# A fused four-block network on one core: the last stage's order of work, rotary buffers and token split rearranged

## The reference, cut to what matters

```python
for i in range(6):
    x = attn_layer(shift_tokens(x), Wqkv[i], q_scale[i], k_scale[i], Wo[i]) + x
    x = ffn_layer(shift_tokens(x), ln_g[i], ln_b[i], W1[i], b1[i], W2[i], b2[i]) + x

def shift_tokens(t):            # the upper 64 channels come from the token before
    a, s = split(t, 2, -1)
    return concat([a, pad(s, one token)[:, :-1]], -1)

def attn_layer(x, Wqkv, qs, ksc, Wo):   # 16 heads of 64, windows of 32 tokens
    q, k, v = heads(x @ Wqkv)
    q, k = l2norm(q) * qs, l2norm(k) * ksc
    q = q * cos * scale + rotate_half(q) * sin * scale
    k = k * cos / scale + rotate_half(k) * sin / scale
    return local_attention(q, k, v) @ Wo     # softmax over own window and the one before
```

## Time and profile before

| | |
|---|---|
| median of three runs | 4209.49 us (4209.45 to 4212.79) |
| the profiled execution, its own time | 4207.12 us |
| its span, first to last instruction | 4205.3 us |
| mean granted clock of TensorE | 0.969 of full |
| TensorE busy (matmuls) | 3880.3 us, 92% |
| VectorE busy | 3528.0 us, 84% |
| ScalarE busy | 2636.6 us, 63% |
| GpSimd busy | 2381.6 us, 57% |

### The profile page before, as it was taken

How to read it: one execution, slowest core, us unless ns; L and a number is a source line. 1 busy time by engine, 2 the same in 40 slices (tenths; PEclk the granted TensorE clock), 3 DMA queues, 4 the chain that set the end, 5 groups by cost and what they waited for, 6 DMA issues and landing times.

```text
span 4205.3 us, 120168 instructions
## 1 busy us (share of the span) xinstructions
PE 3880.3 (92%) x48128; PEld 2725.0 (65%) x48128; DVE 3528.0 (84%) x5537; ACT 2636.6 (63%) x5550; POOL 2381.6 (57%) x2045
## 2 busy tenths in 40 slices
PE   3457998999995999999999999999999999999998
PEld 1225776777774676767776676666766676666765
DVE  6875556777776999999999999999999999999997
ACT  3543336666664666676667666676667666666665
POOL 0111001000002887888878788888878787888885
PEclk7768999999997999999999999999999999999999
DMA  3000000000001333233333333233332333233332
GB/s 105 0 0 1 1 1 1 1 0 0 0 0 41 75 92 82 62 84 89 78 75 70 80 90 82 62 84 91 77 78 67 80 90 82 65 81 75 84 85 65
DMA packets 264675, 238.95 MB, mean 57 GB/s; under 512 B 31716, under 2 KB 260328, under 8 KB 263400
## 3 DMA queue, kind: packets, MB, share of 16 engines
q1 hardware_dynamic: 264168, 231.82, 23.6%
HBM read 26.20 MB, written 4.19 MB: 7 GB/s over the span
## 4 chain that ended last, share of the span: by engine, by line
PE 71%; DVE 13%; ACT 7%; issue 4%; POOL 2%; SPq 2%; DMA 1%; DVEq 0%; ACTq 0%; POOLq 0%
PE bank L1990 13%; PE bank L1923 13%; PE bank L2008 8%; PE bank L1963 7%; PE bank L2050 5%; PE bank L854 4%; ACT arena L1129 3%; PE bank L1956 2%; PE bank L2063 2%; DVE arena L1016 2%; PE bank L1934 2%; DVE arena L1026 2%; PE bank L1254 1%; PE bank L1245 1%; SPq L2169 1%
## 5 line engine op out<-in xcount | busy, mean ns | idle before, releaser
L1451 DVE TENSOR_TENSOR arena<-bank,tab 128x1024 f32<-128x1024 f32 x768 | 935.4, 1218 | 179.7 <-ACT arena L1683 108.0
L1846 POOL TENSOR_TENSOR arena<-arena 128x512 f32<-128x512 f32 x768 | 1011.8, 1333 | 52.1 <-DMA arena<-arena 47.9
L1683 ACT ACTIVATE arena<-bank 128x512 f32<-128x512 f32 x768 | 458.2, 597 | 518.7 <-PE bank L1923 510.0
L1923 PE MATMUL bank<-x_split,wqk_split 128*128 128x256 f32 x4608 | 717.8, 299 | 41.9 <-DVE arena L1451 27.5
L1990 PE MATMUL bank<-m_vo,arena 128*32 128x512 f32 x6144 | 753.9, 597 | 2.1 <-DVE arena L1544 1.1
L1923 PEld LDWEIGHTS bank<-x_split,wqk_split 128*128 128x128 f32 x4608 | 603.5, 191 | 185.5 <-issue 94.4
L1854 POOL TENSOR_TENSOR arena<-arena 128x256 f32<-128x256 f32 x768 | 559.0, 739 | 152.3 <-ACT arena L1683 151.9
L1707 ACT ACTIVATE arena<-bank 128x512 f32<-128x512 f32 x768 | 457.5, 596 | 182.0 <-PE bank L1990 178.9
L1863 POOL TENSOR_TENSOR arena<-arena 128x1024 f32<-128x1024 f32 x192 | 372.8, 1942 | 240.3 <-DVE arena L1499 240.3
L1187 POOL TENSOR_TENSOR x_all<-x_all,arena 128x256 f32<-128x256 f32 x16 | 11.6, 728 | 832.6 <-DVE arena L1008 832.6
L1869 POOL TENSOR_TENSOR arena<-arena 128x1024 f32<-128x1024 f32 x192 | 372.3, 1940 | 122.7 <-DVE arena L1512 122.7
(11 more groups left out here) (258 smaller groups left out, 7115.9 us busy)
## 6 DMA issues: line engine op xcount, KB each, us to landing
arena<-arena SPq DMA_DIRECT2D x1536, 128.0 KB, 2.5
wqk_stage<-in_wqk SPq DMA_DIRECT2D x6, 1024.0 KB, 8.5
out_x<-x_all SPq DMA_DIRECT2D x7, 512.0 KB, 5.0
wvt<-in_wvt SPq DMA_DIRECT2D x6, 512.0 KB, 4.6
wo<-in_wo SPq DMA_DIRECT2D x6, 512.0 KB, 5.7
arena<-in_wbh SPq DMA_DIRECT2D x1, 2048.0 KB, 9.6
w<-in_w SPq DMA_DIRECT2D x6, 341.0 KB, 5.7
wqk_stage<-out_x SPq DMA_DIRECT2D x8, 128.0 KB, 2.4
```

What stands on the lines that cost most here:

```text
L1451: nc.vector.tensor_tensor(d_t[c % KS].rearrange("p k h t -> p k (h t)"), bank[c % 2][:, :].unsqueeze(1).to_broadcast([P, 2, 2 * T]), tab[: ...
L1683: nc.scalar.activation(d_sq[i % 4].rearrange("p h t -> p (h t)"), bank[c % 2][:, :], ACT.Square).then_inc(s_sq, 1)
L1846: nc.gpsimd.tensor_tensor(d_rot[i // 4][:, i % 4, :, :], t[:, :, 0, :], t[:, :, 1, :], ALU.add).then_inc(s_ad, 1)
L1923: last = nc.tensor.matmul(bank[c % 2][:, h * T:(h + 1) * T], wqk_split[:, i, wp, h, :], x_split[:, n % 2, xp, :], start=(q == 0), stop=(q ...
```

## The change

Five things, all in the last stage:

- TensorE's order: `project(f - 1, 5)` comes before `scores(f - 2, 0)`, and `token_products` 0, 1 and 2 stand together before `project(f, 0, 1)`.
- `KS`, the number of rotary buffers, is 4.
- The low half of the tokens is made from bank 6 (PSUM) in two pieces of 64 partitions, the second shifted by a token, at the head of VectorE's turn. It waits until the projections of pass `f - 2` are through. The first column of the second piece is zeroed once, at the start (the eighth of `ZEROS`). `attention(f - 3, 0)`, which writes bank 6, waits for it.
- VectorE's order: rotary product 3 moves to the turn before, product 5 ahead of the first maximum, product 2 ahead of the first softmax sum; the second softmax sum comes behind product 3 and the last residual; the norm's steps stand together.
- ScalarE reads token product 0 before it copies the norm's high half; in the turn of a layer's head matrices the copy comes first. GpSimd's weight splits are spread over the turn, and only two are done in the turn before a new layer.

```diff
--- before.py
+++ after.py
@@ -1316,7 +1316,7 @@
         QUADS = H // 4
         NF = len(FBLK)
         CHUNKS = 8
-        KS = 3
+        KS = 4
         d_xt = [ld(T) for _ in range(3)]
         d_sq = [ld(2, T) for _ in range(4)]
         d_t = [ld(2, 2, T) for _ in range(KS)]
@@ -1353,7 +1353,7 @@
         kept_in = wqk_stage[:, :].rearrange("p (g n c) -> p g n c", g=2, c=C)
         x_kept = [kept_in[:, 0], kept_in[:, 1], wvt[:, :, :], wo[:, :, :]]
         STORES = ((0, 4), (4, 8), (8, 12), (12, 15), (15, 16))
-        ZEROS = 7
+        ZEROS = 8
         TURNS_D = TOTAL + 4
 
         def at_least(eng, s, count):
@@ -1436,8 +1436,12 @@
                 if not here(n):
                     return
                 dve.wait_ge(s_xh, n + 1)
-                nc.vector.tensor_tensor(x_split[:, n % 2, 1, :], d_xt[n % 3], x_split[:, n % 2, 0, :].bitcast(F32), ALU.subtract)\
-                    .then_inc(s_split, 1)
+                at_least(dve, s_proj, CHUNKS * (n - 1))
+                first, second, now = slice(0, C // 2), slice(C // 2, C), n % 2
+                nc.vector.tensor_tensor(x_split[first, now, 1, :], bank[6][first, 0:T],
+                                        x_split[first, now, 0, :].bitcast(F32), ALU.subtract)
+                nc.vector.tensor_tensor(x_split[second, now, 1, 1:], bank[6][second, 0:T - 1],
+                                        x_split[second, now, 0, 1:].bitcast(F32), ALU.subtract).then_inc(s_split, 1)
 
             def rotary_products(n, *chunks):
                 if not here(n):
@@ -1590,6 +1594,7 @@
             nc.vector.scalar_tensor_tensor(d_rstd, d_wn, 1.5, d_rstd, ALU.add, ALU.mult).then_inc(s_stats, 1)
             for v in (*d_xt, d_xf):
                 nc.vector.memset(v, 0.0).then_inc(s_zero, 1)
+            nc.vector.memset(x_split[:, :, 1, 0:1].bitcast(F32), 0.0).then_inc(s_zero, 1)
             dve.wait_ge(s_stats, 8)
             dve.wait_ge(kept, 16 * (NT // KEEP))
             normalise(0)
@@ -1603,38 +1608,38 @@
             dve.wait_ge(s_zero, ZEROS)
             dve.wait_ge(s_stats, 13)
             for f in range(TURNS_D):
+                split_low_tokens(f)
                 turn_probabilities(f - 3, 1)
-                rotary_products(f - 1, 3)
+                rotary_products(f - 1, 4)
                 ffn_gate(f - 4, 0)
-                rotary_products(f - 1, 4)
+                rotary_products(f - 1, 5)
                 softmax_maximum(f - 2, 0)
-                rotary_products(f - 1, 5)
                 softmax_shift(f - 2, 0)
                 rotary_products(f - 1, 6, 7)
                 ffn_gate(f - 4, 1)
+                ffn_gate(f - 4, 2)
                 softmax_maximum(f - 2, 1)
-                split_low_tokens(f)
-                ffn_gate(f - 4, 2)
                 norm_weight(f - 1)
+                norm_factor(f - 1)
+                norm_split(f - 1)
                 residual(f - 3)
-                norm_factor(f - 1)
+                softmax_shift(f - 2, 1)
                 rotary_products(f, 0)
-                norm_split(f - 1)
-                softmax_shift(f - 2, 1)
                 scale_keys(f - 1, 0)
                 rotary_products(f, 1)
                 scale_keys(f - 1, 1)
+                rotary_products(f, 2)
                 softmax_sum(f - 2, 0)
-                rotary_products(f, 2)
                 ffn_weight(f - 3)
                 softmax_reciprocal(f - 2, 0)
                 ffn_factor(f - 3)
                 ffn_scale(f - 3)
-                softmax_sum(f - 2, 1)
-                softmax_reciprocal(f - 2, 1)
+                rotary_products(f, 3)
                 if f - 4 == LAST:
                     add_kept(3, SEQS - 4, SEQS - 1)
                 ffn_residual(f - 4)
+                softmax_sum(f - 2, 1)
+                softmax_reciprocal(f - 2, 1)
                 turn_factors(f - 1)
                 turn_probabilities(f - 2, 0)
                 if f < 2:
@@ -1787,6 +1792,7 @@
             for f in range(TURNS_D):
                 fresh = here(f) and f % SEQS == 0
                 next_fresh = here(f + 1) and (f + 1) % SEQS == 0
+                turned = here(f - 2) and (f - 2) % SEQS == 0
                 read_products(f - 3, 7)
                 read_tokens(f)
                 split_high_tokens(f)
@@ -1807,13 +1813,22 @@
                     weights_high(layer_of(f), 6)
                 nc.scalar.preload_act_table_set(EXP_SET)
                 norm_rsqrt(f - 1)
-                if here(f - 2) and (f - 2) % SEQS == 0:
+                if turned:
                     head_matrices(layer_of(f - 2))
-                softmax_exp(f - 2, 0)
-                squares(f, 0)
-                norm_high(f - 1)
-                read_products(f - 2, 0, 1, 2)
-                squares(f, 1)
+                if turned:
+                    norm_high(f - 1)
+                    squares(f, 0)
+                    softmax_exp(f - 2, 0)
+                    squares(f, 1)
+                    read_products(f - 2, 0, 1, 2)
+                else:
+                    read_products(f - 2, 0)
+                    norm_high(f - 1)
+                    softmax_exp(f - 2, 0)
+                    read_products(f - 2, 1)
+                    squares(f, 0)
+                    read_products(f - 2, 2)
+                    squares(f, 1)
                 if fresh and f:
                     weights_high(layer_of(f), 7)
                 ffn_tokens(f - 3)
@@ -1883,14 +1898,21 @@
                 rotary_sums(f - 1, 5)
                 scale_shifted(f - 2, 0)
                 rotary_sums(f - 1, 6, 7)
+                if fresh:
+                    split_low(pool, layer_of(f), 2, 3)
                 scale_shifted(f - 2, 1)
+                add_halves(f, 0, 1)
                 if fresh:
-                    split_low(pool, layer_of(f), 4, 5, 6, 7)
-                add_halves(f, 0, 1, 2, 3)
+                    split_low(pool, layer_of(f), 4, 5)
+                add_halves(f, 2, 3)
+                if fresh:
+                    split_low(pool, layer_of(f), 6)
                 softmax_scale(f - 2, 0)
+                if fresh:
+                    split_low(pool, layer_of(f), 7)
+                if next_fresh:
+                    split_low(pool, layer_of(f + 1), 0, 1)
                 softmax_scale(f - 2, 1)
-                if next_fresh:
-                    split_low(pool, layer_of(f + 1), 0, 1, 2, 3)
 
         def phase_d_tensor(pe):
             def turn_tokens(n):
@@ -1999,6 +2021,7 @@
                 pe.wait_ge(s_uev, NW * n + 4 * h + 4)
                 if h == 0:
                     pe.wait_ge(s_xt, min(n + 4, TOTAL))
+                    pe.wait_ge(s_split, min(n + 4, TOTAL))
                     if n + 3 > LAST:
                         pe.wait_ge(s_x_done, n - 1)
                 for r in range(QUADS):
@@ -2094,8 +2117,8 @@
                 turn_tokens(f)
                 ffn_up(f - 4, 0)
                 ffn_up(f - 4, 1)
+                project(f - 1, 5)
                 scores(f - 2, 0)
-                project(f - 1, 5)
                 attention(f - 3, 0)
                 project(f - 1, 6)
                 ffn_up(f - 4, 2)
@@ -2108,10 +2131,10 @@
                     head_matrices(layer_of(f - 2))
                     project(f, 0, 1)
                 token_products(f - 2, 0)
+                token_products(f - 2, 1)
+                token_products(f - 2, 2)
                 if not turned:
                     project(f, 0, 1)
-                token_products(f - 2, 1)
-                token_products(f - 2, 2)
                 ffn_tokens(f - 3)
                 spread_norms(f - 1, 0)
                 token_products(f - 2, 3)
```

## The result

The changed kernel takes 4258.98 us (median of 5 runs, 4246.59 to 4267.75), the kernel before 4212.79 us beside it (5 runs, 4209.45 to 4217.12): ratio 1.0106, 95% interval 1.0092 to 1.0120. It is 46 us slower, where 58 us less were forecast. The profiled execution took 4267.75 us, 60.6 more than that of before; its span is 60.7 longer than the earlier trace rows.

What follows compares the result with a forecast made beforehand. A loop over TensorE, VectorE and GpSimd was taken as the bound: 91 turns x 28.68 + 15.7 = 2625.6 us, 58.5 under 2684.06, giving 4148.6 profiled and 4151 median; range 4106 to 4196.

Steps and rivals of the forecast that it cites:

- the third rival: VectorE's norm split misses its place behind GpSimd's sum, making every turn 1.23 us longer: 4263 us, chance 7%.
- S: Start of TensorE's sum of squares in a turn, from which the forecast counted its chain of waits.
- step 4: VectorE from rotary product 2 to the second reciprocal, with the moved operations between: 6.25 us, ending at S + 17.35.
- step 5: GpSimd from the second reciprocal through scaling, rotary sums and halves: 11.26 us, plus 0.07 to hand over.
- The loop: Chain over TensorE, VectorE and GpSimd between successive sums of squares, taken as the new turn: 28.68 us.
- Step 1: TensorE's sum of squares, attention and three token products (0.43, 1.75, three at 0.86); chunk 0 starts at S + 4.76.
- Steps 2 and 3: Chunk 0 to rotary product 0 in 1.57 us, then VectorE's operations and chunk 2's squares; product 2 at S + 11.10.
- The switch at chunk 5 and attention: TensorE's new order avoids slow starts after 32-column products: 0.20 us saved at chunk 5, 0.13 at attention.
- the wait at chunk 4: TensorE's wait for VectorE's rotary product 2 goes: 0.13 + 0.23 = 0.36 us a turn.
- the other 0.33: TensorE's saving from grouped token products (0.13 us) and from tokens' transposes following the projection (0.20).
- The low half: VectorE's two pieces from PSUM take 0.8 us in place of the removed subtraction's 1.35; alone this gains nothing.
- The splits at new layers: GpSimd's spread weight splits give back 2.05 us in each of five new-layer turns: 10.3.

Runs made afterwards that it cites:

- e1: Changed kernel with the norm's weight put in PSUM, so that the factor reads one SBUF tensor: 4240.43 us, ratio 1.0061.
- e11: e5 with TensorE's order as in the kernel before, six stretches of full products: 4240.66 us, ratio 1.0065.
- e5: Changed kernel with the norm's factor and split both reading PSUM, and one more copy on ScalarE: 4186.57 us, ratio 0.9944.
- e10: Kernel before with only the tokens' low half made from PSUM in two pieces, with the zeroed column and attention's wait: 4216.60 us, ratio 1.0014.
- e3: Kernel before with only GpSimd's weight splits in the changed kernel's places: 4202.01 us, ratio 0.9975.
- e4: Changed kernel with the tokens' low half subtracted in one piece from the SBUF copy, at its new place: 4298.08 us, ratio 1.0202.
- e12: Changed kernel with GpSimd's first scaling of scores ahead of rotary sum 5: 4259.85 us, ratio 1.0110.
- e2: Changed kernel with the residual between the norm's weight and factor, so the factor is asked for later: 4262.17 us, ratio 1.0121.
- e8: Changed kernel with GpSimd's rotary sums 6 and 7 waiting for the norm's split: 4232.61 us, ratio 1.0055.

## Why the prediction was wrong, point by point

**The step that failed** is the rejection of the third rival: "Against: 1.35 and 0.45 show that VectorE gets in at the next boundary." The kernel before showed that in each of its turns, and it is no rule. In the change the factor meets GpSimd's queue with 0.6 us of the scaling left and with two sums ready behind it, and is passed over by both in half of the turns (3.36 us for 0.88). The sum had no term for this wait, and only 7% was given to it. That the rival's time (4263) lies near the measured 4259 is luck: it took 1.23 in every turn, and the runs show 1.64 in about half of them and another 0.31 in every turn that has nothing to do with the lock. Its place was one instruction off as well: the factor stalls, while the split stalls only in e1, where the factor no longer does. I had looked at the factor as one that "waits until S + 3.4". It is done at S + 3.26 in the short turn (2120.76 to 2124.02) and at S + 5.74 in the long one.

How the 112.7 us between the forecast's 2625.6 and the 2738.29 divide: 47 long turns at 1.64 are 77; the short turn's length, 28.99 for 28.68, is 91 x 0.31 = 28; the 8 left are four middle turns, the factors of 4.7 and new layers. The 0.31 is 0.24 in steps 1 to 3, 0.03 in step 4 and 0.04 in step 5.

**The loop, step by step,** against the short turn's chain (S = 2120.76):
- Step 1: 4.92 for 4.76. The sum of squares took 0.54 for 0.43 and the three products 2.64 for 2.58.
- Steps 2 and 3: product 0 starts 1.58 behind chunk 0 (1.57 forecast), product 2 another 4.84 later (4.77). Product 2 starts at S + 11.34 for S + 11.10.
- Step 4: from product 2 to the second reciprocal's row in the chain 6.28 (2132.10 to 2138.38, by the turn's period) for 6.25. The price of the moved operations was right.
- Step 5: **one of two paths of the same length.** I followed GpSimd (11.26 + 0.07). It took 11.22: from the reciprocal at 2109.39 to the end of the halves at 2120.61, 0.05 before TensorE's record of the sum begins. But the chain goes over VectorE's own list, from the reciprocal (2109.39) to the end of the first shift (2118.26), 8.87, and then over TensorE's second scores, which wait for that shift: 2.50. Together 11.37. So TensorE's wait was not at the second sum of squares, as forecast, but 2.36 ahead of it. The halves, then the sum:

```profile
2119.18 1.43 POOL L1869 TENSOR_TENSOR arena<-arena 128x256 f32<-128x256 f32 x2
```

```profile
2120.66 0.64 PE L1956 MATMUL bank<-arena,sel 128*32 128x256 f32 x8
```

  I had written "It isn't the bound" of VectorE, with 27.15 busy of 29.21, and did not walk its list from the reciprocal to the shift; a list is a bound through the place at which another engine waits for it, not through its busy share.

The four pieces, 11.34 + 6.28 + 8.87 + 2.50, are the 28.99 of the turn.

**TensorE's order.** The switch at chunk 5 and attention was worth 0.33 as forecast (8.67 to 8.34 up to chunk 7), the wait at chunk 4, 0.36, is gone. From the sum of squares to the tokens' transposes only 0.13 of the other 0.33 came (6.62 to 6.49, medians). Measured in its place within the change (e11 against e5) the order gives 0.52 a turn.

**The low half** cost 0.38 + 0.43 = 0.81 for 0.8:

```profile
L1441 DVE TENSOR_TENSOR x_split<-bank,x_split x96: 375/378/419, 1320.2 to 4159.4; 64x256 fp32r<-64x256 f32 x96
L1443 DVE TENSOR_TENSOR x_split<-bank,x_split x96: 426/427/429, 1320.6 to 4159.8; 64x255 fp32r<-64x255 f32 x96
```

That the removed 1.35 was GpSimd's was right too. That it can turn up at the next instruction with two SBUF operands (e10) I did not say.

**The splits at new layers**: 10.3 forecast, 8.1 measured alone (e3); in the change such a turn is 29.2 where its factor is short (2 of 5) and 32.2 to 32.9 where it is long: there two weight splits stand behind the two sums and pass the factor over as well (4.7 us).

**Four buffers** were put at 0, and no run takes them away alone. By the code, product 3 at its new place would wait with three buffers for GpSimd's sum 0, which stands behind the scaling that needs the reciprocal behind product 3; this was not tried.

**The tail** was put at 0, "between -2 and +3"; it is 4.6 longer.

**What would have shown it**: "A norm split of 0.9 or more with two rotary sums before product 0" was the sign named, and a turn over 29. The turn of 30.63 shows both, the stall one instruction earlier.

## What to carry to other kernels

Where VectorE reads two SBUF tensors while GpSimd has a queue of ready work, price each such instruction at the whole of that queue and not at the rest of one operation; then take the instruction off the pair of SBUF operands (one of them through PSUM: 76.6 us of 2738 here) or leave GpSimd with nothing ready at that moment. When instructions are moved, list every instruction with two SBUF operands and what GpSimd now runs beside it, since a stall removed at one turns up at the next. And a mean hides this: look at minimum, median and maximum of a line, and at the lengths of single turns.

## What the runs showed of the hardware that was not expected

Who gets in when a GpSimd operation ends. The table counts VectorE's requests in the 91 turns; a request is the start of its record. It stands with that much of GpSimd's operation left, and GpSimd's next operation is ready unless said otherwise:

| kernel, instruction | left, us | at the first end | later |
|---|---|---|---|
| before, low half | 1.1 | 91 | 0 |
| e10, factor | 0.9 | 91 | 0 |
| e4, low half | 0.6 (1.2 in two) | 91 | 0 |
| after, factor | 0.6 | 40 | 47 |
| e4, factor | 0.6 | 30 | 58 |
| e12, factor (behind a sum) | 0.6 | 37 | 50 |
| e2, factor | 0.3 | 45 | 41 |
| after, split | 0.3 or less | 37 | 0 |
| before, factor | 0.2 | 91 | 0 |
| e1, split | 0.1 or less | 0 | 76 |
| e8, factor, next sum held by a wait | 0.6 | 88 | 0 |

In the turns missing from a row VectorE asked at another moment, or GpSimd was idle or had nothing ready behind. Two of them, in e2, asked with 0.8 and 0.9 left of a sum and were passed over by the next one; two others, with 0.9 left, were not.

Each stall that lasts ends 0.28 us behind the end of a GpSimd operation. And but for six turns there are two outcomes only: either VectorE gets in at the first end, or it waits until GpSimd has nothing ready: in after, e12, e4, e2 and e1 it was passed over in 281 turns, and in 275 of them GpSimd's next operation began 1.8 us or more behind the one after which VectorE got in. None of the 275 got in between two ready operations, and where two weight splits stood behind the sums they went first too. The other six asked 0.04 us or less before the first end and got in one operation later, with a sum still ready.

It stays open what decides between the two. The time left is not enough: with 0.6 the low half in e4 always got in and the factor in a third to a half of the turns, and with 0.2 to 0.3 the factor of before and the split of after always got in and the factor of e2 in half. The kind of the operation that runs is ruled out by e12. The Trainium skill (SBUF — State Buffer, Who interferes with whom) calls the pair of ports that VectorE and GpSimd share an exclusive lock, and says that the order of issue decides who waits. The lock agrees with the rows: the 0.28, and 0.42 for the same factor with an operand in PSUM (e1). The order of issue does not fit the long factors, as far as records show it: the factor's record starts 0.55 us before that of the first sum (2181.12 and 2181.67), and both sums go first.

The second surprise is e8: an engine made to wait 180 us in all, with nothing else changed, made the kernel faster.
